# Wide-head attention of a four-layer decoder: four score banks, and the turning of a tile moved ahead of the product before it

## The chip, the cores and the metric

One core of a Trainium2 chip runs the whole program. The metric is the device time of one execution in microseconds. TensorE multiplies matrices, VectorE and ScalarE read its results out of PSUM (8 banks of 128 partitions x 512 float32), GpSimd does small side work, and SyncE starts the DMA transfers.

## The reference, cut to what matters

Twelve sublayers (attention, cross attention and feed-forward, four times) act on four sequences of 512 tokens of width 256. Four of them hold an attention whose head is "wide", that is a single head over 256 or 64 columns. All four have this core, in float32:

```python
scores = jnp.einsum('bqd,bkd->bqk', q, k) * scale      # 512 x 512 for each sequence
scores = jnp.where(mask, scores, -inf)                 # causal, by valid keys, or no mask
attn = jax.nn.softmax(scores, axis=-1)
y = jnp.einsum('bqt,btd->bqd', attn, v)
```

`L0_attn` is causal with width 256, `L0_ffn` is causal with width 64 (its attention sits between a mixture of projections and a mixture of outputs), `L1_xattn` has no mask and width 256, and `L3_xattn` masks keys and has width 256.

## The kernel before, in words

The program walks over the four sequences ("batches") one after another: nine early sublayers and the routing of the tenth for each batch, then a routed expert stage for all, then the last three sublayers for each batch. Every stage is a block in which each engine has its own instruction list and all engines meet at the end of the block; so a block lasts as long as its longest chain. `wide_attention` is one such block. It is called in `L0_attn`, `L0_ffn`, `L1_xattn` and `L3_xattn`, for 4 batches, so 16 times in all.

In a call, the 512 queries are four tiles t = 0 to 3 of 128 rows. `span[t]` is the number of keys that a tile looks at: 512, or 128, 256, 384 and 512 for the causal callers. For a tile there are six steps:

- the scores, on TensorE (line 354): one or two float32 products into PSUM bank t % 2. The trace shows a float32 product as two instructions, so a tile of width 256 has four, each with its load of the stationary side;
- the maximum of each row, on VectorE (line 384 without a mask, 395 with one; for `L3_xattn` line 389 multiplies by the key mask first). With a mask it also writes the masked scores into SBUF;
- the exponential with the row sum, on ScalarE (line 420), from the bank or from the masked scores, into `probs`;
- the turning (TensorE transposes of 128x128, line 366) of the tile's `span[t]`/128 chunks of `probs` into bank 2 + t % 2;
- the copy of that bank into `probs_t`, on VectorE (line 405);
- the product with the values, on TensorE (line 374), into bank 4 + t % 2, two instructions for each chunk, and then the finish on VectorE, which divides by the sum (line 408 has made its reciprocal) and adds or stores (lines 809, 977, 1034, 1957 in the callers).

Below, s0 to s3 are the scores, T0 to T3 the turnings and W0 to W3 the products with the values. `probs`, `scores`, `kept` and `probs_t` have two buffers each. The order is written out by hand. TensorE's list reads s0 s1 T0 W0 s2 T1 W1 s3 T2 W2 T3 W3. VectorE's reads maximum 0, maximum 1, copy 0, finish 0, maximum 2, copy 1, finish 1, maximum 3, copy 2, finish 2, copy 3, finish 3. Each W waits for its copy, and the copy of tile t stands on VectorE behind the maximum of tile t + 1:

```python
score(0)
for t in range(NT):
    if t + 1 < NT:
        score(t + 1)
    pe.wait_ge(probs_done, t + 1)      # then the turning of tile t
    ...
    pe.wait_ge(copied_done, t + 1)     # then its product with the values
```

After the block come a block of the caller or the next `layernorm`, which starts the load of the weights of the sublayer after it.

Of the kernel before, what the change touches and what calls it, by code (L numbers as in the profile page):

```python
# [21 lines left out]
ALU = mybir.AluOpType  # L22
ACT = mybir.ActivationFunctionType
AX = mybir.AxisListType

B, T, D, P = 4, 512, 256, 128
NT, NC = T // P, D // P
# [295 lines left out]

def wide_attention(net, q, k, values, width, causal, finish, keep=None, gone=None):

    masked = causal or keep is not None  # L330
    with ExitStack() as ctx:
        probs = net.sbuf("probs", [P, 2, T], ctx=ctx)
        scores = net.sbuf("scores", [P, 2, T], ctx=ctx) if masked else None
        kept = net.sbuf("kept", [P, 2, T], ctx=ctx) if keep is not None else None
        probs_t = net.sbuf("probs_t", [P, 2, T], ctx=ctx)
        nmax = net.sbuf("nmax", [P, NT], ctx=ctx)
        total = net.sbuf("total", [P, NT], ctx=ctx)
        inverse = net.sbuf("inverse", [P, NT], ctx=ctx)
        span = [(t + 1) * P if causal else T for t in range(NT)]
        with net.block() as (block, sem):  # L340
            scores_done, kept_done, max_done, probs_done = sem("scores"), sem("kept"), sem("maximum"), sem("exp")
            turned_done, copied_done, out_done = sem("transposed"), sem("transpose copied"), sem("p @ v")
            inverse_done, tile_done = sem("1/sum"), sem("tile written")

            @block.tensor
            def _(pe):
                def score(t):
                    if t >= 2:
                        if masked:
                            pe.wait_ge(max_done, t - 1)  # L350
                        else:
                            pe.wait_ge(probs_done, t - 1)
                    for i, (a, b) in enumerate(zip(q, k)):
                        mm = pe.matmul(net.psum[:, t % 2, 0:span[t]], a[:, t * P:(t + 1) * P], b[:, 0:span[t]],  # L354
                                       start=i == 0, stop=i == len(q) - 1)
                    mm.then_inc(scores_done, 1)

                score(0)
                for t in range(NT):
                    if t + 1 < NT:  # L360
                        score(t + 1)
                    pe.wait_ge(probs_done, t + 1)
                    if t >= 2:
                        pe.wait_ge(copied_done, t - 1)
                    for c in range(span[t] // P):
                        mm = pe.transpose(net.psum[:, 2 + t % 2, c * P:(c + 1) * P],
                                          probs[:, t % 2, c * P:(c + 1) * P], net.ident)
                    mm.then_inc(turned_done, 1)
                    pe.wait_ge(copied_done, t + 1)
                    if t >= 2:  # L370
                        pe.wait_ge(tile_done, t - 1)
                    n = span[t] // P
                    for c in range(n):
                        mm = pe.matmul(net.psum[:, 4 + t % 2, 0:width], probs_t[:, t % 2, c * P:(c + 1) * P],
                                       values(c), start=c == 0, stop=c == n - 1)
                    mm.then_inc(out_done, 1)

            @block.vector
            def _(dve):
                def maximum(t):  # L380
                    dve.wait_ge(scores_done, t + 1)
                    src = net.psum[:, t % 2, 0:span[t]]
                    if not masked:
                        dve.tensor_reduce(nmax[:, t:t + 1], src, AX.X, ALU.max, negate=True).then_inc(max_done, 1)
                        return
                    if t >= 2:
                        dve.wait_ge(probs_done, t - 1)
                    if keep is not None:
                        dve.tensor_tensor(kept[:, t % 2, :], src, keep, ALU.mult).then_inc(kept_done, 1)
                        dve.wait_ge(kept_done, t + 1)  # L390
                        src, mask = kept[:, t % 2, :], gone
                    else:
                        mask = net.causal[:, BANK - span[t]:BANK]

                    dve.tensor_tensor_reduce(scores[:, t % 2, 0:span[t]], src, mask, -1.0, 3e38, ALU.add, ALU.min,
                                             nmax[:, t:t + 1]).then_inc(max_done, 1)

                maximum(0)
                for t in range(NT):
                    if t + 1 < NT:  # L400
                        maximum(t + 1)
                    dve.wait_ge(turned_done, t + 1)
                    if t >= 2:
                        dve.wait_ge(out_done, t - 1)
                    dve.tensor_copy(probs_t[:, t % 2, 0:span[t]], net.psum[:, 2 + t % 2, 0:span[t]])\
                       .then_inc(copied_done, 1)
                    dve.wait_ge(probs_done, t + 1)
                    dve.reciprocal(inverse[:, t:t + 1], total[:, t:t + 1]).then_inc(inverse_done, 1)
                    dve.wait_ge(inverse_done, t + 1)
                    dve.wait_ge(out_done, t + 1)  # L410
                    finish(dve, t, net.psum[:, 4 + t % 2, 0:width], inverse[:, t:t + 1]).then_inc(tile_done, 1)

            @block.scalar
            def _(act):
                for t in range(NT):
                    act.wait_ge(max_done, t + 1)
                    if t >= 2:
                        act.wait_ge(turned_done, t - 1)
                    src = scores[:, t % 2, 0:span[t]] if masked else net.psum[:, t % 2, 0:span[t]]
                    act.activation(probs[:, t % 2, 0:span[t]], src, ACT.Exp, bias=nmax[:, t:t + 1],  # L420
                                   scale=-1.0 if masked else 1.0, accum_out=total[:, t:t + 1]).then_inc(probs_done, 1)

def stack_pairs(net, jobs, qs, ks, v, values, vbias, rope=None):
# [352 lines left out]
def L0_attn(net, W, x, xn, xc, **_):  # L779

    with ExitStack() as ctx:
# [26 lines left out]
        def finish(dve, t, ps, inverse):  # L808
            return dve.scalar_tensor_tensor(out=x[:, t, :], in0=ps, scalar=inverse, in1=x[:, t, :],
                                            op0=ALU.mult, op1=ALU.add)  # L810
        wide_attention(net, [q[:, c, :] for c in range(NC)], [k[:, c, :] for c in range(NC)],
                       lambda c: v[:, c, :], D, True, finish)

# [5 lines left out]
def L0_ffn(net, W, x, xn, xc, parts, **_):  # L819

    with ExitStack() as ctx:
# [154 lines left out]
        def finish(dve, t, ps, inverse):  # L976
            return dve.tensor_scalar(attn[:, t, :], ps, inverse, None, ALU.mult)
        wide_attention(net, [qk[:, 0, :]], [qk[:, 1, :]], lambda c: qkv[:, c, 2, :], MIXD, True, finish)

        mixed = lasting("mixed", [P, 2, MIX, MIXD])  # L980
# [38 lines left out]
def L1_xattn(net, W, x, xn, xc, cc, **_):  # L1019

    with ExitStack() as ctx:
        q = net.sbuf("q", [P, NC, T], ctx=ctx)
        k = net.sbuf("k", [P, NC, T], ctx=ctx)
        v = net.sbuf("v", [P, NT, D], ctx=ctx)
        o = net.sbuf("o", [P, NC, D, 2], ctx=ctx)
        table = []
        for c in range(NC):
            table.append(cols_out("dve", W["wq"], D, xc, c * P, q[:, c, :], ("scalar", W["bq"][:, c:c + 1], D ** -0.5, ALU.add, ALU.mult)))
            table.append(cols_out("act", W["wk"], D, cc, c * P, k[:, c, :], ("act", ACT.Identity, W["bk"][:, c:c + 1], 1.0)))
        table += [rows_out(alternate(t), cc, t, W["wv"], D, 0, D, v[:, t, :], copied(alternate(t)), W["bv"]) for t in range(NT)]  # L1030
        products(net, table)

        def finish(dve, t, ps, inverse):
            return dve.tensor_scalar(o[:, t % 2, :, t // 2], ps, inverse, None, ALU.mult)
        wide_attention(net, [q[:, c, :] for c in range(NC)], [k[:, c, :] for c in range(NC)],
                       lambda c: v[:, c, :], D, False, finish)
        add_output(net, x, o[:, :, :, :].rearrange("p c f r -> p c (f r)"), NC, P, W["wo"])
# [1407 lines left out]
```

## Time and profile before

| | |
|---|---|
| three runs | 4296.89, 4298.70 (median), 4308.47 us |
| the profiled execution | 4299.54 us, span of its instructions 4297.7 us |
| TensorE busy, loads busy | 79%, 50% of the span |
| VectorE, ScalarE, GpSimd busy | 48%, 27%, 9% |
| mean granted TensorE clock | 0.888 of full speed |

No engine is busy all the time; the program is a chain of blocks. The busy shares are means over blocks with different limits, so a block has to be read by itself: in the timeline of one call, and in the table of busy times by stretch, which also gives the granted TensorE clock (1.00 is 2.4 GHz, 0.50 is 1.2 GHz; a stretch with both lies between).

### The profile page before, as it was taken

Reading aid. Unit: us, or ns where it says so; the run is one execution under the profiler, and the core shown is the slowest. Engines: PE = TensorE matmul, PEld = TensorE weight load, DVE = VectorE, ACT = ScalarE, POOL = GpSimd, SP = SyncE. Lnnn points to the kernel's source line nnn. Section 1 sums busy time; section 2 is a strip of 40 time slices with the busy share of each in tenths; the row PEclk is TensorE's granted clock in tenths of the full one; section 3 lists DMA queues with packets and bytes.
Section 4 is the critical chain, followed back from the end, with each engine's and each line's share of the span. In section 5 each row is a group of like instructions: output and inputs, shape, how many; then the busy total and the mean of one; then the engine's idle time right before and its main releaser. Section 6 shows DMA issues by size and latency. Waiting matters only on the chain. (4 is left out here: it accounts for less than half of the span.)

```text
span 4297.7 us, 49457 instructions
## 1 busy us (share of the span) xinstructions
PE 3401.4 (79%) x18289; PEld 2170.2 (50%) x18289; DVE 2078.9 (48%) x4553; ACT 1146.9 (27%) x2199; POOL 401.3 (9%) x381
## 2 busy tenths in 40 slices
PE   4778689678869967887986778798595888877888
PEld 3364555436455544645454455544593454454545
DVE  3655445465545546555555654554113435344353
ACT  1413125141223414122341312243131213112121
POOL 0010101010010101001010100101102000010100
PEclk9888899888889978898997979899797998989989
DMA  4000100200010010001001000100682110102011
GB/s 163 13 13 21 63 11 1 86 13 13 21 63 11 17 70 13 13 20 63 11 28 59 13 13 23 61 10 33 246 306 97 51 41 7 78 8 84 8 51 38
DMA packets 53212, 209.27 MB, mean 49 GB/s; under 512 B 4977, under 2 KB 37617, under 8 KB 41329
## 3 DMA queue, kind: packets, MB, share of 16 engines
q1 hardware_dynamic: 48128, 198.85, 12.5%
q0 software_dynamic: 1536, 4.20, 0.3%
q8 instruction: 157, 2.57, 0.2%
q10 hardware_dynamic: 3312, 3.02, 0.2%
q14 instruction: 79, 0.64, 0.0%
HBM read 186.89 MB, written 19.16 MB: 48 GB/s over the span
## 5 line engine op out<-in xcount | busy, mean ns | idle before, releaser
L643 DVE TENSOR_REDUCE nmax<-psum 128x1 f32<-128x512 f32 (+3 forms) x768 | 392.2, 553 | 135.6 <-PE psum L579 91.5
L685 ACT ACTIVATE probs<-psum 128x1024 f32<-128x1024 f32 (+3 forms) x384 | 304.4, 814 | 431.0 <-PE psum L607 290.0
L108 PE MATMUL psum<-select 128*128 128x512 f32 x1016 | 280.2, 431 | 82.9 <-PEq L120 82.9
L574 PE MATMUL psum<-ks,qs 64*128 64x512 f32 (+3 forms) x768 | 211.1, 546 | 139.5 <-DVE nmax L643 123.5
L108 PEld LDWEIGHTS psum<-select 128*128 128x128 f32 x1016 | 205.3, 208 | 156.9 <-issue 113.3
L316 ACT ACTIVATE xc<-psum 128x256 f32<-128x256 f32 x152 | 54.5, 389 | 790.1 <-PE psum L309 790.1
L265 POOL TENSOR_SCALAR rstd<-mean_var 128x4 f32<-128x4 f32 x48 | 10.9, 228 | 2491.5 <-DVE mean_var L290 2491.5
L574 PEld LDWEIGHTS psum<-ks,qs 64*128 64x128 f32 x768 | 89.0, 227 | 290.2 <-DVE nmax L643 269.5
L1490 ACT ACTIVATE exps<-exps,nmax 128x512 f32<-128x512 f32 x256 | 183.4, 717 | 71.4 <-DVE nmax L1436 71.0
L1436 DVE CUSTOM_DVE_ANT_0 exps<-psum,mrows 128x512 f32<-128x512 f32 x256 | 166.1, 689 | 67.9 <-PE psum L1383 64.6
L602 PE MATMUL psum<-qs,ks 64*128 64x512 f32 (+3 forms) x768 | 165.0, 435 | 7.8 <-ACT probs L685 7.8
L618 PE MATMUL psum<-probs,v 128*32 128x512 f32 (+3 forms) x1536 | 166.4, 506 | 3.3 <-ACT probs L685 2.5
L1394 PE MATMUL psum<-consts,exps 128*128 128x128 f32 x1024 | 138.9, 279 | 3.8 <-DVE arena L1444 1.5
L1394 PEld LDWEIGHTS psum<-consts,exps 128*128 128x128 f32 x1024 | 109.5, 141 | 55.9 <-ACT exps L1490 39.8
L1405 PE MATMUL psum<-arena,v 128*64 128x512 f32 x512 | 134.8, 608 | 3.6 <-ACT arena L1503 3.2
L746 DVE RECIPROCAL inv<-psum 128x512 f32<-128x512 f32 x16 | 53.7, 3358 | 166.8 <-PE psum L721 166.8
L2045 PE MATMUL psum<-xc,arena 128*128 128x512 f32 x256 | 123.6, 606 | 4.1 <-PEq L120 4.1
L354 PE MATMUL psum<-k,q 128*128 128x512 f32 (+3 forms) x192 | 92.9, 625 | 37.8 <-PEq L120 37.8
L738 PE MATMUL psum<-arena,scaled 128*128 128x256 f32 x512 | 120.0, 382 | 0.0
L293 DVE TENSOR_SCALAR xn<-x,mean_var,rstd 128x256 f32<-128x256 f32 x192 | 85.3, 508 | 70.7 <-POOL rstd L267 70.7
L199 PE MATMUL psum<-arena,proj 128*128 128x256 f32 x512 | 111.5, 380 | 5.8 <-PEq L120 5.8
L738 PEld LDWEIGHTS psum<-arena,scaled 128*128 128x128 f32 x512 | 96.0, 190 | 38.0 <-issue 15.3
(371 smaller groups left out, 6700.9 us busy)
## 6 DMA issues: line engine op xcount, KB each, us to landing
arena<-in_w SPq DMA_DIRECT2D x23, 1028.0 KB, 5.0
arena<-in_w SPq DMA_DIRECT2D x23, 1024.0 KB, 5.2
arena<-in_pack_L_ffn SPq DMA_DIRECT2D x4, 5184.5 KB, 15.5
arena<-in_pack_L_xattn SPq DMA_DIRECT2D x4, 4744.0 KB, 13.9
arena<-in_pack_L_ffn SPq DMA_DIRECT2D x4, 4120.0 KB, 13.1
arena<-in_pack_L_attn SPq DMA_DIRECT2D x5, 2432.0 KB, 9.2
arena<-in_pack_L_attn SPq DMA_DIRECT2D x9, 1280.0 KB, 5.5
arena<-ternary SPq DMA_DIRECT2D x4, 2056.0 KB, 7.8
```

What stands on the lines that cost most here:

```text
L108: pe.matmul(self.psum[:, bank, :], self.select[:, 0, :], self.select[:, 0:BANK // P, :], start=True, stop=True)
L574: mm = pe.matmul(net.psum[:, bank_of(s + j), 0:w], qs[half, p, qt * P:(qt + 1) * P], ks[half, p, 0:w], start=True, stop=not causal)
L602: mm = pe.matmul(net.psum[:, 2 + 2 * (n % 2) + j, lo:T], ks[half, p, kt * P:(kt + 1) * P], qs[half, p, lo:T], start=True, stop=not causal)
L618: mm = pe.matmul(net.psum[u * PITCH:(u + 1) * PITCH, 6, lo:T], v[:, kt, 4 * g + u, :], probs[:, (2 * m + u // 2) % buffers, u % 2, lo:T], ...
L643: dve.tensor_reduce(nmax[:, p, qt, n % 2:n % 2 + 1], net.psum[:, bank_of(s), 0:w], AX.X, ALU.max, negate=True).then_inc(row_read, 1)
L685: act.activation(probs[:, n % buffers, :, lo:T], net.psum[:, first:first + 2, lo:T], ACT.Exp, scale=scale)\
L738: mm = pe.matmul(net.psum[:, 4 + t, 0:D], scaled[:, c, t * P:(t + 1) * P], w[:, c * D:(c + 1) * D], start=c == 0, stop=c == GROUPS - 1)
L1394: mm = pe.transpose(net.psum[:, 4 + j, kt * P:(kt + 1) * P], e[:, m % ring, kt * P:(kt + 1) * P], net.ident)
L1405: mm = pe.matmul(net.psum[half, 6, :], v[:, kt, 2 * p + j, :], turned[p % 2][:, kt, j, :], start=kt == 0, stop=kt == NT - 1, tile_position ...
L1436: dve.tensor_tensor_reduce(e[:, m % ring, :], net.psum[:, 2 * (u % 2) + j, :], mrows[:, u % NT, :], -DK ** -0.5, 1e20, ALU.add, ALU.min, n ...
L1490: act.activation(e[:, m % ring, :], e[:, m % ring, :], ACT.Exp, bias=nmax[:, m % ring:m % ring + 1], scale=-1.0, accum_out=total[:, p % 2, ...
L2045: mm = pe.matmul(net.psum[:, n % 2, :], W["down"][:, at:at + P], xc[:, c, :], start=c == 0, stop=c == 1)
```

## The change

- The scores of the four tiles have a bank each (0, 1, 6 and 7), so the waits of the scores for a free bank are gone. `probs` and `scores` have four buffers in place of two, so the waits of the exponential and of the maximum for a free buffer are gone (of the latter the masked product, `kept`, keeps one, on VectorE itself).
- TensorE's list becomes s0 s1 s2 s3 T0 T1 W0 T2 W1 T3 W2 W3.
- VectorE's list becomes maximum 0 to 3, copy 0, copy 1, finish 0, copy 2, finish 1, copy 3, finish 2, finish 3.
- The number and shapes of the instructions that compute stay as they are. `probs_t` and the banks 2 to 5 stay doubled, with their waits.

```diff
-                def score(t):
-                    if t >= 2:
-                        if masked:
-                            pe.wait_ge(max_done, t - 1)
-                        else:
-                            pe.wait_ge(probs_done, t - 1)
...
+                    for i, (a, b) in enumerate(zip(q, k)):
+                        mm = pe.matmul(net.psum[:, score_banks[t], 0:span[t]], a[:, t * P:(t + 1) * P], b[:, 0:span[t]],
...
-                score(0)
-                for t in range(NT):
-                    if t + 1 < NT:
-                        score(t + 1)
+                def turn(t):
                     pe.wait_ge(probs_done, t + 1)
                     if t >= 2:
                         pe.wait_ge(copied_done, t - 1)
...
+                def weigh(t):
                     pe.wait_ge(copied_done, t + 1)
                     if t >= 2:
                         pe.wait_ge(tile_done, t - 1)
...
+                for t in range(NT):
+                    score(t)
+                turn(0)
+                for t in range(NT):
+                    if t + 1 < NT:
+                        turn(t + 1)
+                    weigh(t)
...
-                maximum(0)
-                for t in range(NT):
-                    if t + 1 < NT:
-                        maximum(t + 1)
+                def copy(t):
                     dve.wait_ge(turned_done, t + 1)
                     if t >= 2:
                         dve.wait_ge(out_done, t - 1)
...
+                for t in range(NT):
+                    maximum(t)
+                copy(0)
+                for t in range(NT):
+                    if t + 1 < NT:
+                        copy(t + 1)
                     dve.wait_ge(probs_done, t + 1)
...
-                    if t >= 2:
-                        act.wait_ge(turned_done, t - 1)
```

## Rows read from the trace of the kernel before

**Rows 1.** Calls by stretch: us, busy PE, PEld, DVE, ACT, POOL (instructions), PEclk, DMA, GB/s.

```profile
71.12:85.95 14.83, 11.25 (x46) 7.42 (x46) 5.86 (x20) 2.62 (x8) 0.00 (x0) 1.00 0.01 2
809.60:827.20 17.60, 14.06 (x46) 9.13 (x46) 5.70 (x20) 2.62 (x8) 0.00 (x0) 0.81 0.00 0
...
274.50:290.60 16.10, 13.29 (x38) 8.10 (x38) 5.36 (x20) 2.62 (x8) 0.00 (x0) 0.50 0.00 0
...
436.44:457.55 21.11, 16.93 (x64) 10.62 (x64) 7.37 (x16) 3.12 (x8) 0.00 (x0) 1.00 0.00 0
...
3413.24:3438.75 25.51, 19.23 (x64) 11.42 (x64) 10.19 (x24) 3.26 (x8) 0.00 (x0) 0.91 0.00 1
```

**Rows 2.** Waits by who waited for whom: total us, times, longest us.

```profile
PEld psum L374 <- DVE probs_t L405: 75.3, 64, 1.9
```

**Rows 3.** Timeline, a call of L1_xattn: start, us, engine, line, op [idle before <-releaser].

```profile
438.47 0.69 DVE L384 TENSOR_REDUCE nmax<-psum 128x1 f32<-128x512 f32 x1 [2.31 <-PE psum L354]
...
440.18 0.69 DVE L384 TENSOR_REDUCE nmax<-psum 128x1 f32<-128x512 f32 x1 [1.02 <-PE psum L354]
440.79 0.68 DVE L405 COPY probs_t<-psum 128x512 f32<-128x512 f32 x1
...
441.52 1.59 PEld L374 LDWEIGHTS psum<-v,probs_t 128*128 128x128 f32 x8 [1.08 <-DVE probs_t L405]
...
443.14 0.41 PEld L354 LDWEIGHTS psum<-k,q 128*128 128x128 f32 x2
...
443.64 0.48 DVE L1034 TENSOR_SCALAR o<-psum,inverse 128x256 f32<-128x256 f32 x1 [2.10 <-PE psum L374]
...
451.71 1.59 PEld L374 LDWEIGHTS psum<-v,probs_t 128*128 128x128 f32 x8 [1.18 <-DVE probs_t L405]
...
453.33 0.57 PEld L366 LDWEIGHTS psum<-consts,probs 128*128 128x128 f32 x4
...
454.95 1.59 PEld L374 LDWEIGHTS psum<-v,probs_t 128*128 128x128 f32 x8 [1.05 <-DVE probs_t L405]
```

**Rows 4.** Timeline, a call of L3_xattn.

```profile
3419.16 0.69 DVE L389 TENSOR_TENSOR kept<-psum,keep 128x512 f32<-128x512 f32 x1 [0.68 <-PE psum L354]
...
3420.51 0.69 DVE L405 COPY probs_t<-psum 128x512 f32<-128x512 f32 x1
...
3421.24 1.59 PEld L374 LDWEIGHTS psum<-ct,probs_t 128*128 128x128 f32 x8 [1.45 <-DVE probs_t L405]
...
3436.15 1.59 PEld L374 LDWEIGHTS psum<-ct,probs_t 128*128 128x128 f32 x8 [1.04 <-DVE probs_t L405]
```

**Rows 5.** Timeline, the first call of L0_attn.

```profile
72.74 0.43 DVE L395 CUSTOM_DVE_ANT_0 scores<-psum,consts 128x256 f32<-128x256 f32 x1 [0.57 <-PE psum L354]
...
73.12 0.29 DVE L405 COPY probs_t<-psum 128x128 f32<-128x128 f32 x1
...
73.47 0.30 PEld L374 LDWEIGHTS psum<-v,probs_t 128*128 128x128 f32 x2 [0.57 <-DVE probs_t L405]
...
83.36 1.59 PEld L374 LDWEIGHTS psum<-v,probs_t 128*128 128x128 f32 x8 [1.04 <-DVE probs_t L405]
```

**Rows 6.** The start of its second call by stretch, columns as in Rows 1.

```profile
809.90:816.70 6.80, 6.29 (x16) 3.90 (x16) 1.49 (x7) 1.09 (x4) 0.00 (x0) 0.50 0.00 1
```

**Rows 7.** Timeline, the first call of L0_ffn.

```profile
276.18 0.42 DVE L395 CUSTOM_DVE_ANT_0 scores<-psum,consts 128x256 f32<-128x256 f32 x1 [0.55 <-PE psum L354]
...
286.20 0.87 PEld L366 LDWEIGHTS psum<-consts,probs 128*128 128x128 f32 x4
...
288.25 1.78 PEld L374 LDWEIGHTS psum<-qkv,probs_t 128*128 128x128 f32 x8 [1.18 <-DVE probs_t L405]
```

**Rows 8.** The block after that call: its transposes in the timeline.

```profile
292.22 6.46 PE L1000 MATMUL psum<-consts,mixed 128*128 128x128 f32 x32 [2.00 <-DVE mixed L990]
```

**Rows 9.** Stretches of that block and behind it, columns as in Rows 1.

```profile
292.20:297.90 5.70, 5.68 (x27) 5.66 (x28) 3.55 (x3) 3.26 (x6) 0.00 (x0) 0.50 0.00 0
297.90:301.00 3.10, 2.11 (x13) 1.77 (x12) 0.00 (x0) 1.42 (x3) 0.00 (x0) 1.00 0.02 5
```

More of the change, by code:

```diff
@@ L330, in wide_attention @@
     masked = causal or keep is not None
+    score_banks = (0, 1, 6, 7)
     with ExitStack() as ctx:
-        probs = net.sbuf("probs", [P, 2, T], ctx=ctx)
-        scores = net.sbuf("scores", [P, 2, T], ctx=ctx) if masked else None
+        probs = net.sbuf("probs", [P, NT, T], ctx=ctx)
+        scores = net.sbuf("scores", [P, NT, T], ctx=ctx) if masked else None
         kept = net.sbuf("kept", [P, 2, T], ctx=ctx) if keep is not None else None
@@ L347, in score @@
                 def score(t):
-                    if t >= 2:
-                        if masked:
-                            pe.wait_ge(max_done, t - 1)
-                        else:
-                            pe.wait_ge(probs_done, t - 1)
                     for i, (a, b) in enumerate(zip(q, k)):
-                        mm = pe.matmul(net.psum[:, t % 2, 0:span[t]], a[:, t * P:(t + 1) * P], b[:, 0:span[t]],
+                        mm = pe.matmul(net.psum[:, score_banks[t], 0:span[t]], a[:, t * P:(t + 1) * P], b[:, 0:span[t]],
                                        start=i == 0, stop=i == len(q) - 1)
                     mm.then_inc(scores_done, 1)
-                score(0)
-                for t in range(NT):
-                    if t + 1 < NT:
-                        score(t + 1)
+                def turn(t):
                     pe.wait_ge(probs_done, t + 1)
@@ L365, in _ @@
                     for c in range(span[t] // P):
-                        mm = pe.transpose(net.psum[:, 2 + t % 2, c * P:(c + 1) * P],
-                                          probs[:, t % 2, c * P:(c + 1) * P], net.ident)
+                        mm = pe.transpose(net.psum[:, 2 + t % 2, c * P:(c + 1) * P], probs[:, t, c * P:(c + 1) * P], net.ident)
                     mm.then_inc(turned_done, 1)
+                def weigh(t):
                     pe.wait_ge(copied_done, t + 1)
@@ L381, in maximum @@
                     dve.wait_ge(scores_done, t + 1)
-                    src = net.psum[:, t % 2, 0:span[t]]
+                    src = net.psum[:, score_banks[t], 0:span[t]]
                     if not masked:
@@ L385, in maximum @@
                         return
-                    if t >= 2:
-                        dve.wait_ge(probs_done, t - 1)
                     if keep is not None:
+                        if t >= 2:
+                            dve.wait_ge(max_done, t - 1)
                         dve.tensor_tensor(kept[:, t % 2, :], src, keep, ALU.mult).then_inc(kept_done, 1)
@@ L393, in maximum @@
                         mask = net.causal[:, BANK - span[t]:BANK]
-                    dve.tensor_tensor_reduce(scores[:, t % 2, 0:span[t]], src, mask, -1.0, 3e38, ALU.add, ALU.min,
+                    dve.tensor_tensor_reduce(scores[:, t, 0:span[t]], src, mask, -1.0, 3e38, ALU.add, ALU.min,
                                              nmax[:, t:t + 1]).then_inc(max_done, 1)
-                maximum(0)
-                for t in range(NT):
-                    if t + 1 < NT:
-                        maximum(t + 1)
+                def copy(t):
                     dve.wait_ge(turned_done, t + 1)
@@ L416, in _ @@
                     act.wait_ge(max_done, t + 1)
-                    if t >= 2:
-                        act.wait_ge(turned_done, t - 1)
-                    src = scores[:, t % 2, 0:span[t]] if masked else net.psum[:, t % 2, 0:span[t]]
-                    act.activation(probs[:, t % 2, 0:span[t]], src, ACT.Exp, bias=nmax[:, t:t + 1],
+                    src = scores[:, t, 0:span[t]] if masked else net.psum[:, score_banks[t], 0:span[t]]
+                    act.activation(probs[:, t, 0:span[t]], src, ACT.Exp, bias=nmax[:, t:t + 1],
                                    scale=-1.0 if masked else 1.0, accum_out=total[:, t:t + 1]).then_inc(probs_done, 1)
```

## The prediction

> **What bounds the kernel now.** I read the table by stretch first, cut at the 16 calls of the changed block, to see how long the calls are, at which clock they run and whether one engine fills them. Four rows stand for the four callers, and one more for the case in which the clock differs [rows 1]: about 14.8 us for `L0_attn` (two of its four calls; the other two last 17.6), 16.1 for `L0_ffn`, 21.1 for `L1_xattn`, 25.5 for `L3_xattn`. Weighted by four calls each that is about 316 us, 7% of the program; the change can touch only these. Within a call no engine is full. In the `L1_xattn` call TensorE is busy 16.93 of 21.11 us, VectorE 7.37, ScalarE 3.12.
>
> The waits by who waited for whom then name the idle stretches: all 64 products with the values wait for the copy of their turned tile, 75.3 us in total [rows 2]. The timeline of one call shows why [rows 3]. Copy 0 starts at 440.79, right behind maximum 1 (440.18), although the turned tile had been ready; W0 follows 0.73 us after the copy's start. Only after W0 do the scores of tile 2 go out (443.14), since they stand behind it in TensorE's list. So in each round TensorE runs scores and turning, stops for maximum and copy, and runs the product. The chain that ends the block is s0, s1, maximum 1, copy 0, W0, s2, T1, maximum 2, copy 1, W1 and so on: TensorE work and VectorE work in a row, not side by side.
>
> **The change part by part.** Everything after the load of W3 (its product, the last finish, the end of the block) is as before. So I work out, for one call of each caller, when W3 starts to load, and compare it with the old start.
>
> *The scores moved ahead.* Four scores without a break: a tile of 512 keys and width 256 takes 1.71 us, the distance of maximum 1 from maximum 0 (440.18 - 438.47) [rows 3]. All four maxima now stand ahead of copy 0 on VectorE, and this is the wait that the change adds: behind copy 0 in the queue stands everything else of VectorE, and W0 waits for it. Its cost is in the walk below, as W0 starts later than before. The exponentials run on ScalarE, which is busy 3.12 us of the call, beside this.
>
> *The turning moved ahead of the product.* Each turning of four chunks loads in 0.57 us, eight loads of a product take 1.62 us to the next instruction (451.71 to 453.33) [rows 3]. Once W0 has started, the list T2 W1 T3 W2 W3 runs on if every copy is in time. Copy 2 stands behind finish 0, and finish t starts 2.12 us after its product began to load (441.52 to 443.64) and takes 0.48; then 0.73 from copy to load: 3.33 us after W0, whereas W2 comes 1.62 + 0.57 + 1.62 + 0.57 = 4.38 after W0. Copy 3 in the same way: 3.33 after W1, whereas W3 comes 1.62 + 0.57 + 1.62 = 3.81 after it. So TensorE has no wait, with 0.5 us to spare at the tightest place for 512 keys. In the causal callers, whose early tiles are short, the room is about 0.1 us.
>
> *`L1_xattn`* [rows 3]: maximum 3 starts at 438.47 + 3 x 1.71 = 443.60. Copy 0 follows 0.61 later (as 440.79 follows 440.18), at 444.21, and W0 0.73 later, at 444.94. T0 and T1, 1.14 us together, lie beside that. From W0 to W3: three products and two turnings, 3 x 1.62 + 2 x 0.57 = 6.00, so W3 at 450.94 in place of 454.95. Gain 4.0 us.
>
> *`L3_xattn`* [rows 4]: VectorE needs 1.35 us for a tile's mask product and maximum (3419.16 to 3420.51), less than the 1.71 of a score, so scores set the pace. The mask product of tile 3 starts at 3419.16 + 2 x 1.71 = 3422.58, copy 0 at 3423.93, W0 0.73 later at 3424.66, W3 at 3430.66 in place of 3436.15. Gain 5.5 us.
>
> *`L0_attn`* [rows 5]: maximum 1 at 72.74. Tile 2 has three quarters of the columns (1.28, an estimate from the 1.71), tile 3 all: maximum 3 at 75.73. Copy 0 at + 0.61 = 76.34, W0 at + 0.35 (73.12 to 73.47) = 76.69. Up to W3 there are 2 + 4 + 6 = 12 loads of products at 1.62 / 8 and 3 + 4 = 7 of turnings at 0.57 / 4: 3.43. W3 at 80.12 in place of 83.36. Gain 3.2 us. Two of the four calls have half the clock over 6.8 us from their start [rows 6], which makes them 17.60 - 14.83 = 2.8 longer [rows 1]; I let the loss stand and give them the same gain.
>
> *`L0_ffn`* runs at half the clock all through [rows 1]. A single product for a tile's scores (width 64) at half the clock costs as two at full, so again 1.28 and 1.71 for tiles 2 and 3: maximum 3 at 276.18 + 2.99 = 279.17 [rows 7], W0 0.61 + 0.35 later at 280.13. The loads take 0.22 here (1.78 / 8 and 0.87 / 4 [rows 7]): 19 x 0.22 = 4.18. W3 at 284.31 in place of 288.25. Gain 3.9 us.
>
> *Costed at nothing*: the waits dropped (TensorE's for a score bank, ScalarE's for a buffer) take no engine time; their stalls are in the walk. The wider buffers add no instruction. No DMA is moved in the list; the next weights are asked for one sublayer ahead, by the `layernorm` that now starts 3 to 6 us sooner. If a load were late by that, the gain of the call would be lost, but no more.
>
> Sum: 4 x (4.0 + 5.5 + 3.2 + 3.9) = 66.4 us. From the profiled 4299.5 that leaves 4233; the median of the three runs is 0.8 us lower, so **4232 us**. What is late next in the call: W0, which waits for maximum 3 and copy 0 (TensorE idle some 0.3 us in `L1_xattn`, 1.3 in `L3_xattn`), and behind it TensorE itself.
>
> *The clock, bounded from both sides.* No row shows a call in the new order. Upwards: `L0_ffn` could come to full clock since TensorE no longer pauses. 27 loads from W0 on and 32 transposes of the next block, which take 6.46 us [rows 8], would go from 0.22 and 0.20 to about 0.14 (0.57 / 4): 2.2 + 1.9 us a call, 16 in all. Downwards: the shift of all later work can put a half-clock stretch where there was none; it costs 2.8 us each [rows 1], and eight more of them 22 us. I take nothing, as three of the four callers are at 0.91 to 1.00 in most rows [rows 1]. These bounds give 4216 and 4254.
>
> A rule against the change: 5.70 us in which TensorE ran nothing but transposes began at clock 0.50 and were followed by 1.00 [rows 8, 9], so transposes count as work for the clock here. The Trainium skill, "TensorE: Matmul & The Clock Gate", section "Part 4: PE-mode transpose", says otherwise: full rate does not engage for transposes, since they don't count as busy in the same way. By the row the sum stays; by the page it would be the rival "clock lost" below. The trace disagrees with the page.
>
> **The rivals.**
> - *Clock gain*, 4216: the upper bound above. For it: TensorE's list in `L0_ffn` runs without a pause from W0 to W3. Against: after the call there is a pause of 2.0 us [rows 8] that stays.
> - *The VectorE chain*, 4268: if W2 and W3 came only after finish, copy and load of the tiles before (2.12 + 0.48 + 0.73 = 3.33 a step in place of 2.19), two steps lose 2.3 a call, 36 in 16 calls. For it: finish 0 stands ahead of copy 2. Against: W1 lies between, with the room worked out above.
> - *Clock lost between s3 and W0*, 4266: only T0, T1 and the idle time lie there; if they dropped the clock, each of the 12 calls at full clock would lose 2.8 us, 34 in all. Against: in the old order TensorE pauses over a microsecond before each W [rows 3] at clock 1.00.
> - *Slower*, 4313: the clock falls at the same place and stays at half up to the end of the call. W0 to W3 would double: 7.62 in eight calls and 5.05 in four, together 81 us, 14 more than the gain. It decides from the point where over 66 / 81 = 82% of these stretches are at half. Against: the known half stretch ends after 6.8 us although TensorE pauses within it [rows 6].
> - *Nothing*, 4299: a wait that isn't in the trace keeps the old rounds. Nothing in the diff would do so.
>
> **How the numbers follow.** Forecast 0.72, clock gain 0.12, VectorE chain 0.07, clock lost 0.03, slower 0.03, nothing 0.03. The forecast's own range is 4218 to 4248 (the walk within 10%, and some half-clock stretches more or fewer); with the bounds of the clock the range is 4210 to 4254, which leaves out the last four cases, 0.16. About 0.3%, 13 us, is what a measurement of this kernel can tell from no change: faster 0.94 (the first four), same 0.03, slower 0.03.
>
> **What would show it.** In the profile after, a call of `L1_xattn` should last about 17.1 us, of `L3_xattn` 20.0, of the shorter `L0_attn` 11.6 and of `L0_ffn` 12.2. Copy 0 should stand right behind maximum 3, W0 should be the only product that waits for its copy, so the total of that wait should fall from 75 us to some 20, and four scores should go out at 1.71 a tile. It would be wrong if W2 or W3 wait for their copies, if the clock row of the calls falls below that of before, or if the time goes back in the blocks behind the calls.

## The result, and the profile after

The changed kernel takes 4219.39 us (median; 4217.98 to 4224.96), the kernel before took 4296.89 beside it; the ratio is 0.9818, with a 95% interval of 0.9803 to 0.9833. That is 77.5 us less, where 66.4 were forecast: 4219.4 in place of 4232, inside the range of 4210 to 4254. The profiled execution took 4219.39 us, its span is 4217.6 and its mean granted clock 0.892.

The same view by stretch as in [rows 1], of the kernel after (stretch, its length, busy time of PE, PEld, DVE, ACT, POOL with instructions, clock, DMA): two calls of `L0_attn`, then one each of `L0_ffn`, `L1_xattn` and `L3_xattn`, each cut after its last finish.

```profile
70.64:83.85 13.21, 11.92 (x46) 8.51 (x46) 5.81 (x20) 2.62 (x8) 0.00 (x0) 0.87 0.00 1
797.89:811.10 13.21, 11.92 (x46) 8.63 (x46) 5.81 (x20) 2.62 (x8) 0.00 (x0) 0.87 0.00 1
272.62:284.44 11.82, 11.25 (x38) 8.38 (x38) 5.21 (x20) 2.62 (x8) 0.00 (x0) 0.50 0.00 0
429.18:446.35 17.17, 16.03 (x64) 10.67 (x64) 7.38 (x16) 3.11 (x8) 0.00 (x0) 1.00 0.00 0
3360.26:3380.45 20.19, 18.32 (x64) 11.58 (x64) 10.18 (x24) 3.26 (x8) 0.00 (x0) 0.88 0.01 1
```

TensorE now fills the calls: in `L1_xattn` it is busy 16.03 of 17.17 us, where it was 16.93 of 21.11 [rows 1]. VectorE and ScalarE do the same work as before. The wait of [rows 2], 75.3 us in 64 pieces, has become this row of the waits view (total, times, longest):

```profile
PEld psum L364 <- DVE probs_t L400: 14.8, 16, 1.5
```

One wait is left in each call, that of W0. The timeline of a call of `L1_xattn`, to be held against [rows 3] (start, length, engine, line, operation; in brackets the idle time before it and what ended it):

```profile
431.20 0.69 DVE L382 TENSOR_REDUCE nmax<-psum 128x1 f32<-128x512 f32 x1 [2.31 <-PE psum L346]
...
436.35 0.69 DVE L382 TENSOR_REDUCE nmax<-psum 128x1 f32<-128x512 f32 x1 [1.02 <-PE psum L346]
436.96 1.28 DVE L400 COPY probs_t<-psum 128x512 f32<-128x512 f32 x2
...
437.69 1.59 PEld L364 LDWEIGHTS psum<-v,probs_t 128*128 128x128 f32 x8 [0.74 <-DVE probs_t L400]
...
439.31 0.57 PEld L355 LDWEIGHTS psum<-consts,probs 128*128 128x128 f32 x4
...
439.86 1.60 PEld L364 LDWEIGHTS psum<-v,probs_t 128*128 128x128 f32 x8
...
441.48 0.58 PEld L355 LDWEIGHTS psum<-consts,probs 128*128 128x128 f32 x4
441.97 0.48 DVE L1032 TENSOR_SCALAR o<-psum,inverse 128x256 f32<-128x256 f32 x1 [1.01 <-PE psum L364]
442.02 3.32 PEld L364 LDWEIGHTS psum<-v,probs_t 128*128 128x128 f32 x16
...
442.37 0.68 DVE L400 COPY probs_t<-psum 128x512 f32<-128x512 f32 x1
```

Maximum 3 starts 5.15 us after maximum 0 (three tiles at 1.72), copy 0 stands right behind it, W0 follows 0.73 later, and from there T2, W1, T3, W2 and W3 load without a break. The copies come in time: copy 3 starts at 442.37 and would let W3 load at 443.10, and TensorE comes to W3 at 442.02 + 1.62 = 443.64.

For what follows, a call is counted from the load of its first score to the end of its last product, in the timeline. The 16 calls sum to 307.6 us before and 240.9 after, 66.7 less. The rest of the span goes from 3990.1 to 3976.7, 13.4 less, although its instructions are the same. So two things are to be explained: which part of the change gives the 66.7, and where the 13.4 come from.

### The profile page after: what moved, and what is told of

The parts are those of the page before. It is cut to its first block and busy times, and to the rows that moved or that the text cites. A ratio compares the mean times of both kernels' runs of the same rounds, so it can differ in the third digit from the quotient of the medians.

```text
span 4217.6 us, 49409 instructions
## 1 busy us (share of the span) xinstructions
PE 3372.7 (80%) x18289; PEld 2170.9 (51%) x18289; DVE 2078.1 (49%) x4553; ACT 1146.6 (27%) x2199; POOL 401.5 (10%) x381
## 3 DMA queue, kind: packets, MB, share of 16 engines
q1 hardware_dynamic: 48128, 198.85, 12.6%
```

## The experiments

A series is a set of runs taken together; the kernel before ran in each, with medians of 4296.9 to 4305.6 us, and the ratios are to it. This table has the medians (single times for three), the sum of the calls and the rest of the span in the profile:

| kernel | time, us | 16 calls | rest |
|---|---|---|---|
| before (two profiles) | 4296.9, 4294.5 | 307.6, 307.4 | 3990.1, 3988.7 |
| after (two profiles) | 4219.4, 4223.1 | 240.9, 240.9 | 3976.7, 3979.8 |
| scores first, turning not ahead | 4274.8 | 295.6 | 3980.8 |
| turning ahead, two score banks | 4222.2 | 236.6 | 3985.0 |
| after, end of `L3_xattn` 1.2 us later | 4231.3 (single) | 238.8 | 3990.5, of which 4.9 added |
| after, end of `L3_xattn` 2.4 us later | 4237.8 (single) | 240.2 | 3995.8, of which 9.8 added |
| after, more VectorE work ahead of the copies | 4231.1 (single), 4232.4 | 244.3, 244.3 | 3984.8, 3988.7 |
| after, with dummy products ahead | 4202.7 | 211.2 | 3986.0 |
| turning ahead, two banks, dummy products | 4206.2 | 223.9 | 3978.3 |
| after, more dummy products | 4190.8 | 207.0 | 3981.7 |
| turning ahead, two banks, more dummy products | 4202.3 | 211.7 | 3986.9 |

### Scores first, without the turning ahead

```diff
-                turn(0)
                 for t in range(NT):
-                    if t + 1 < NT:
-                        turn(t + 1)
+                    turn(t)
                     weigh(t)
...
-                copy(0)
                 for t in range(NT):
-                    if t + 1 < NT:
-                        copy(t + 1)
+                    copy(t)
```

> Four score banks as in the change, but each tile is turned, copied and weighed in turn: T0 W0 T1 W1 T2 W2 T3 W3, and VectorE has copy t, finish t. Theory (the turning moved ahead carries the gain): copy t+1 now stands behind finish t, so a round is 2.12 + 0.48 + 0.73 = 3.33 us at 512 keys, and W3 starts 9.99 us after W0 in place of 6.00. L1_xattn then ends where it did before, L3_xattn 1.5 us sooner, L0_ffn 0.7, L0_attn about even: some 8 us less than before in all, about 4289, within 10 us for the clock. Rival (the scores in four banks carry it): at least half of the 77 us stay, 4258 or less.

Measured: 4274.77 us, ratio 0.9939 (0.9918 to 0.996), 26 us less than before. The calls give 12.0 of it, against some 8 expected: `L3_xattn` 1.7 a call, `L0_ffn` 0.9, `L1_xattn` 0.3, `L0_attn` 0.1 in the mean. The total was missed, because the rest of the span was 9 us shorter too; the rival, at least half of the gain, was missed as well. The timeline of its `L1_xattn` call shows the round that was worked out:

```profile
445.10 1.59 PEld L364 LDWEIGHTS psum<-v,probs_t 128*128 128x128 f32 x8 [1.18 <-DVE probs_t L398]
...
447.21 0.48 DVE L1028 TENSOR_SCALAR o<-psum,inverse 128x256 f32<-128x256 f32 x1 [2.10 <-PE psum L364]
447.61 0.68 DVE L398 COPY probs_t<-psum 128x512 f32<-128x512 f32 x1
...
448.34 1.59 PEld L364 LDWEIGHTS psum<-v,probs_t 128*128 128x128 f32 x8 [1.05 <-DVE probs_t L398]
```

Product, finish, copy, product: 3.24 us a round, with TensorE's loads idle over a microsecond before each W. Four banks alone leave this chain as it is.

### The turning ahead, with two score banks

On the kernel before, with its buffers and waits; VectorE's list in the same order (maximum 0, 1, copy 0, then maximum t + 2, copy t + 1, finish t).

```diff
-                score(0)
-                for t in range(NT):
-                    if t + 1 < NT:
-                        score(t + 1)
+                score(0)
+                score(1)
+                turn(0)
+                for t in range(NT):
+                    if t + 2 < NT:
+                        score(t + 2)
+                    if t + 1 < NT:
+                        turn(t + 1)
+                    weigh(t)
```

> Two score banks and two buffers with all waits of the kernel before, but the turning moved ahead of the product: s0 s1 T0 s2 T1 W0 s3 T2 W1 T3 W2 W3, VectorE maximum 0, 1, copy 0, maximum 2, copy 1, finish 0, maximum 3, copy 2, finish 1, copy 3, finish 2, 3. Theory (the order matters, not the banks): the scores of tile 2 fill TensorE while copy 0 runs, W3 of L1_xattn starts 14.2 us after the first score in place of 14.5 after the change, L3_xattn is the same, L0_attn and L0_ffn gain 0.3 to 0.5 a call: 4215, within 6. Rival (two banks hold the order up): a wait for a bank or buffer comes back, at least 2 us a call, 4250 or more.

Measured: 4222.17 us, ratio 0.9817 (0.9797 to 0.9838); the changed kernel in the same series 0.9824 (0.9803 to 0.9845). So the order gives the whole gain, and the four banks are not needed for it. The orders of TensorE and VectorE were changed together; no run has one without the other. The calls are 4.3 us shorter than after the change, as expected in sum (the time missed the range of 4209 to 4221 by 1 us), though not caller by caller: `L1_xattn` 15.9 in place of 16.6, `L3_xattn` 18.9 in place of 19.6 and `L0_attn` 12.0 in place of 12.6 in the mean, but `L0_ffn` 12.3 in place of 11.4. The rest of the span took the gain back. In `L3_xattn` turnings wait for their exponential here, as in this row of T3:

```profile
3376.77 0.42 PEld L363 LDWEIGHTS psum<-consts,probs 128*128 128x128 f32 x4 [0.60 <-ACT probs L435]
```

### Both kernels once more

> The changed kernel once more. In the first profiles the 16 calls (first score load to the end of the last product) sum to 307.6 us before and 240.9 after, a gain of 66.7; the rest of the span is 3990.1 and 3976.7, a gain of 13.4 that lies outside the calls. Theory (where the half-clock stretches fall outside the calls differs from one execution to the next): the calls repeat within 3 us, the rest moves by 5 us or more. Rival (the shorter calls make the blocks behind them faster each time): the rest comes out at 3976.7 within 2 us.

> The kernel before once more. Theory (half-clock stretches outside the calls differ from one execution to the next): the calls sum to 307.6 within 4 us, the rest moves by 5 us or more from 3990.1. Rival (a steady difference): the rest is 3990.1 within 2 us.

Measured: 4223.09 and 4294.53 us. The sums of the calls agree within 0.2 us. The rest is 3979.8 in place of 3976.7, and 3988.7 in place of 3990.1. It moves by 3.1 after the change and by 1.4 before it, less than the 5 us that luck was to bring; the 3.1 are more than the rival's 2 us.

Two profiles of a kernel that come out alike don't show that nothing is drawn. In the series of these runs the executions of the kernel before take 4289 to 4309 us. Its four `L0_attn` calls last 14.24, 17.12, 17.12 and 14.24 us in one profile and 18.25, 14.24, 15.43 and 15.51 in the other, so that the sums agree is chance. And the two kernels of the next section differ from the changed kernel only from the first `L3_xattn` call on. Up to it, the changed kernel (twice) and these two run the same instructions, but the views by stretch are 7.7 us apart:

```profile
0.00:3360.26 3360.26, 2656.67 (x14673) 1721.48 (x14673) 1711.38 (x3740) 965.66 (x1878) 340.40 (x320) 0.89 0.14 52
0.00:3363.49 3363.49, 2658.87 (x14673) 1720.76 (x14674) 1711.29 (x3740) 965.29 (x1878) 340.08 (x320) 0.89 0.14 52
0.00:3365.61 3365.61, 2662.14 (x14673) 1723.85 (x14673) 1711.25 (x3740) 965.39 (x1878) 340.03 (x320) 0.89 0.14 52
0.00:3367.94 3367.94, 2668.15 (x14673) 1729.05 (x14674) 1711.17 (x3740) 965.71 (x1878) 340.11 (x320) 0.88 0.14 52
```

Outside the calls TensorE is at half the clock there for 697, 711, 718 and 728 us by the clock record, in the order of the lengths. So over this part of the program the theory is borne out: the same instructions got more or less half clock from one execution to another. (The four come from three series, which may add to it.)

The part from the first `L3_xattn` call on does repeat. Outside its calls it takes 784.5 and 784.1 us before and 778.9 and 778.8 after, and the timeline shows where the 5.5 us lie. In a block behind each `L3_xattn` call a chain on VectorE takes 11.4 us while TensorE runs 36 products beside it; then TensorE turns VectorE's result and runs five more products, for which the rest of the block waits. Before the change a half-clock stretch falls on these products in some calls and ahead of the chain in the others, and either costs about 1.4 us; one of them is so in each of the eight calls of both profiles. After the change it falls, in all eight, on the products beside VectorE, where it costs nothing. (With the turning ahead and two score banks it falls on the five products in all four calls, and this part takes 784.1 us again.) The five products behind the first of these calls, before and after:

```profile
3462.38:3465.90 3.52, 3.52 (x5) 1.67 (x6) 0.00 (x0) 1.25 (x2) 0.00 (x0) 0.56 0.00 0
3404.07:3406.06 1.99, 1.99 (x5) 1.02 (x6) 0.00 (x0) 1.24 (x2) 0.00 (x0) 1.00 0.00 0
```

So of the 13.4 us outside the calls some 5.5 are steady. The other 8 lie ahead of the first `L3_xattn` call, where the changed kernel's own instructions spread as widely.

### The end of a call later

Behind the last finish of the `L3_xattn` calls, with n = 2 and n = 4:

```diff
+                for i in range(late):
+                    dve.tensor_copy(probs[:, i, :], net.psum[:, 2, :])
```

> The changed kernel, with two more VectorE copies of a bank behind the last finish of the L3_xattn calls (4 of the 16), 1.2 us in all, that nobody reads. From the first score of one such call to that of the next it took 255.8 to 256.0 us before, 252.6 with the scores first alone and 249.2 after, so the steps are 3.4 us although the calls themselves became 1.7 and 5.4 shorter. Theory (the half-clock stretches in the blocks behind the call take up the difference, since where they fall depends on when the call ends): the time from call to call stays at 249.2 or goes to 252.6, and isn't 250.4. Rival (the rest is the same from call to call, whatever the call does): 249.2 + 1.2 = 250.4.

> The same with four more copies, 2.4 us. Theory: the time from call to call is 252.6 (or still 249.2). Rival: 251.6.

Measured, from call to call: 249.28, 249.18 and 252.02 us with 1.2 us added; 252.38, 250.95 and 251.02 with 2.4 added. Adding 1.2 us costs nothing twice and 2.8 us once; adding 2.4 costs 3.2 once and 1.8 twice. The changed kernel has 248.97 to 249.24 in six such ways, so the rest isn't the same whatever the call does. Of the values that I expected, 249.2 and 252.6, four of the six are near; the two at 251.0 are neither these nor the rival's 251.6, so the rule of fixed steps fell. The total times, 4231.27 and 4237.77, are no price of the later end: each is of a single run, and 5.4 and 7.7 us of its distance to the first profile of the changed kernel lie ahead of the first edited instruction.

### More VectorE work in the chain of the copies

```diff
                 def copy(t):
+                    if t >= 2:
+                        dve.tensor_tensor(extra[:, :], net.causal, net.causal, ALU.add)
                     dve.wait_ge(turned_done, t + 1)
```

> The changed kernel with one more VectorE operation of 512 columns (0.61 us to the next) ahead of copy 2 and of copy 3 in every call, in the chain from a finish through the copy to the next product; its output is read by nobody. Theory (TensorE sets the end of the call, VectorE has room: after the change copy 2 of L1_xattn is through 1.1 us before TensorE comes to W2, copy 3 0.5 before W3): L1_xattn and L3_xattn become 0.1 us longer a call, L0_ffn 0.1, L0_attn 0.5. Rival (the VectorE chain sets the end): both copies come 0.61 later and each call is 1.2 us longer.

> The changed kernel with one more VectorE operation ahead of copy 2 and copy 3, once more, with rounds. In its profile the calls were 3.4 us longer than after the change (all of it in L0_attn), the rest of the span 5.0 to 8.1 us longer although the instructions there are the same. Theory (the end of a call decides where half-clock stretches fall behind it, in the same way in every execution): the median is again some 10 us above that of the changed kernel, 4229 to 4233, and the rest 3984 within 2. Rival (the rest is luck of one execution): the median is 3.4 us above, 4223 to 4226, and the rest 3978.

Measured: `L1_xattn` 16.57 and `L0_ffn` 11.44 us a call as without it, `L3_xattn` between 19.50 and 19.64, and `L0_attn` 0.86 longer (13.47). The room in the chain is there as worked out, and used up only in `L0_attn`: W2 of it now waits for its copy (it doesn't in the changed kernel):

```profile
808.12 0.55 DVE L403 COPY probs_t<-psum 128x384 f32<-128x384 f32 x1
808.72 1.16 PEld L365 LDWEIGHTS psum<-v,probs_t 128*128 128x128 f32 x6 [0.33 <-DVE probs_t L403]
```

The time, however, is 4231.11 us, and 4232.38 (4231.14 to 4234.87) in the second series: some 10 us above the changed kernel in other series, and not 3.4. These 10 us aren't clear of noise. The ratio to the kernel before is 0.984 (0.9824 to 0.9857), and the changed kernel's own 0.9818 and 0.9824 have intervals that overlap it; and in the first of these two series the kernels of the section above need as long as this one outside the calls, 3204.8 and 3205.4 us against 3205.9 up to the first `L3_xattn` call. In the second series the rest was to be 3984 within 2 and is 3988.7, a miss.

What does show clearly is one part of it, the way from an `L0_attn` call to the next `L0_ffn` call. Behind the second to fourth calls it lasts 190.4 to 190.7 us here, in six of six, and 188.3 to 189.2 in the four profiles of the kernels whose call ends as after the change, in twelve of twelve. Before the change it is 190.1 to 190.4 in three of eight and 188.6 to 189.1 in the others. Three kernels, the same instructions behind the second call, in three stretches by the same offsets (before, after, this one):

```profile
826.73:834.00 7.27, 4.60 (x20) 2.98 (x20) 4.84 (x14) 1.09 (x3) 3.48 (x5) 0.99 0.78 290
834.00:841.00 7.00, 5.93 (x15) 4.83 (x16) 0.52 (x2) 0.77 (x2) 1.83 (x3) 0.53 0.71 304
841.00:1017.00 176.00, 133.54 (x611) 79.16 (x609) 121.10 (x205) 53.20 (x65) 19.71 (x8) 0.86 0.02 8
```

```profile
810.51:817.80 7.29, 4.62 (x20) 2.98 (x20) 4.85 (x14) 1.09 (x3) 3.49 (x6) 1.00 0.78 296
817.80:824.10 6.30, 5.24 (x17) 4.41 (x18) 0.51 (x2) 0.77 (x2) 1.82 (x3) 0.73 0.76 330
824.10:998.80 174.70, 132.20 (x608) 78.44 (x608) 121.08 (x205) 53.20 (x65) 19.73 (x8) 0.86 0.02 8
```

```profile
813.13:820.42 7.29, 4.64 (x21) 2.98 (x20) 4.85 (x14) 1.09 (x3) 3.49 (x6) 0.99 0.77 287
820.42:828.00 7.58, 6.51 (x17) 5.24 (x18) 0.51 (x2) 0.77 (x2) 1.82 (x3) 0.56 0.66 283
828.00:1003.50 175.50, 133.10 (x608) 78.67 (x607) 121.03 (x205) 53.19 (x65) 19.72 (x8) 0.86 0.02 8
```

In the second stretch TensorE has 15 to 17 products. It runs them at a mean clock of 0.73 in the changed kernel, and at 0.53 and 0.56 in the other two, and the stretch takes 6.30 us against 7.00 and 7.58. (The stretch of the kernel before is cut two instructions shorter.) That is 1.3 of the 2.1 us between the changed kernel and this one; the other 0.8 lie in the third stretch. The stretch at half the clock itself, in the changed kernel and in this one:

```profile
818.55:821.96 3.41, 3.10 (x7) 2.53 (x8) 0.00 (x0) 0.38 (x1) 1.11 (x2) 0.50 1.05 454
820.33:827.16 6.83, 5.67 (x13) 4.49 (x14) 0.60 (x2) 0.56 (x2) 1.83 (x3) 0.50 0.73 314
```

The call ended 0.86 us later, and the half clock behind it lasts twice as long. This holds throughout: of the 40 such ways in the ten profiles without added dummy products, the 29 with 3.4 us at half the clock behind the call last 188.3 to 189.5 us, and the 11 with 6.8 us last 190.1 to 191.1.

### Dummy products ahead of the calls

TensorE idles in the blocks ahead of `L0_attn`, `L0_ffn` and `L3_xattn`; here it multiplies there, into a bank that nobody reads: 10 products in the rotation of `L0_attn`, 30 behind the projections of `L0_ffn`, 14 while `L3_xattn` makes its masks.

```diff
+            @block.tensor
+            def _(pe):
+                net.keep_warm(pe, 10)
...
+                net.keep_warm(pe, 30, bank=0, after=(weighed_done, 20))
...
+                net.keep_warm(pe, 14)
```

> The changed kernel with dummy products on TensorE in the three blocks ahead of calls where TensorE has nothing to do: 10 in the rotation of L0_attn, 30 at the end of the projections of L0_ffn, 14 while L3_xattn makes its masks. Their results are read by nobody. Theory (the calls of these three lose time to the half clock with which they begin): L0_attn 11.0 us from the first score to the end of the last product in place of 12.6, L0_ffn about 8.7 in place of 11.4, L3_xattn 17.4 in place of 19.6, together 26 us less in 12 calls, and with the turning ahead of and behind L0_ffn some 33: about 4188. Rival (the clock at the start of a call is of no account, since VectorE and ScalarE set the pace there): the calls as they are, 4220.

Measured: 4202.70 us, ratio 0.978 (0.9757 to 0.9804). `L0_attn` takes 10.93 us in all four calls and `L3_xattn` 17.31, as expected (11.0 and 17.4); `L0_ffn` 6.93 in three calls, less than the 8.7 expected, and 11.11 in one. The calls lose 29.7 us against the changed kernel. The rest is 9 us longer than in its first profile, and the total was missed by 15; part of the 9 may be the series, in which the same instructions up to the first `L3_xattn` call took 5 to 8 us longer than in that profile. The odd call and its neighbour in the view by stretch show what is different, the clock:

```profile
992.60:1004.11 11.51, 10.92 (x38) 8.06 (x38) 5.22 (x20) 2.62 (x8) 0.00 (x0) 0.52 0.00 0
271.31:278.64 7.33, 6.28 (x38) 4.66 (x38) 5.07 (x20) 2.62 (x8) 0.00 (x0) 1.00 0.00 0
```

> Both findings together: two score banks with the order s0 s1 T0 s2 T1 W0 s3 T2 W1 T3 W2 W3, and dummy products ahead of the calls of L0_attn, L0_ffn (33 in place of 30, since one of the four calls there had still begun at half the clock) and L3_xattn. Theory (the gains of the calls add up): from the first score to the end of the last product L1_xattn 15.9 us, L0_attn 10.9, L0_ffn 7, L3_xattn 16.9, together 203 in place of the 211.2 of the dummy products alone; the rest of the span at 3986 as there gives 4190, within 8 for the half-clock stretches elsewhere. Rival (the order of the two lists doesn't matter once the clock is full, since VectorE then sets the pace): 211 in the calls, 4199.

Measured: 4206.22 us (ratio 0.9781, 0.9765 to 0.9798), a miss. Three callers came out as expected (15.90, 10.94 and 17.09 us), but `L0_ffn` began at the full clock and fell back to half in all four calls, 11.9 to 12.2 us each, for 224 in the calls in place of 203. The two last kernels try the pause that was left, with five more products in the block that turns the queries and keys of `L0_ffn` (`warm=5` there):

```diff
-def products(net, table, name="products"):
+def products(net, table, name="products", warm=0):
...
+            net.keep_warm(pe, warm)
```

> The changed kernel with the dummy products of e5_warm (10, 30, 14), and 5 more in the block that turns the queries and keys of L0_ffn, where TensorE waits some 2 us for ScalarE between its transposes and the first scores. Theory (that pause let the clock fall in one call of four): all four calls of L0_ffn last 6.9 us, the calls sum to 207, and the time is some 5 us below that of e5_warm, 4198, within 6. Rival (the clock falls for another reason): again one or more calls of L0_ffn at 11 us, 4203.

> The order with two score banks (s0 s1 T0 s2 T1 W0 s3 T2 W1 T3 W2 W3) and the same dummy products (10, 30, 5, 14). Theory: L0_ffn at full clock, about 7 us a call in place of 12, the calls sum to 203, some 20 us less than in e6_turn_ahead_warm, 4186, within 8. Rival (in this order TensorE pauses at the head of the L0_ffn call, which lets the clock fall whatever stands ahead): L0_ffn again near 12 us, 4206.

Measured: on the changed kernel 4190.81 us, ratio 0.9745 (0.9715 to 0.9774), with all four `L0_ffn` calls at 6.93 us and the calls at 207.0, as expected; the time is 1 us below the range of 4192 to 4204. It is the fastest of all. One odd call in four against none is thin evidence for the pause as the cause; the other order shows more, where the calls lasted 11.9 to 12.2 us without the five products. On the other order 4202.29 us (0.9767, 0.9745 to 0.979) in place of 4186: `L0_ffn` 8.35, 10.75, 8.35 and 8.50 us. Two of them by stretch:

```profile
273.31:282.05 8.74, 6.90 (x38) 4.62 (x38) 5.20 (x20) 2.62 (x8) 0.00 (x0) 1.00 0.01 2
994.84:1005.98 11.14, 10.17 (x38) 7.19 (x38) 5.29 (x20) 2.62 (x8) 0.00 (x0) 0.64 0.00 0
```

The rival has a part in the second, where the clock fell to half within the call (0.64 over it). But the first is at 1.00 and still takes 8.74 us, 1.4 more than with four scores in a row (7.32 below): with scores between the turnings the short tiles of `L0_ffn` leave pauses. The four callers in the fastest kernel, by stretch:

```profile
71.94:83.47 11.53, 10.23 (x46) 7.42 (x46) 5.81 (x20) 2.62 (x8) 0.00 (x0) 1.00 0.00 1
273.51:280.83 7.32, 6.28 (x38) 4.65 (x38) 5.07 (x20) 2.62 (x8) 0.00 (x0) 1.00 0.00 0
426.75:443.92 17.17, 16.03 (x64) 10.67 (x64) 7.38 (x16) 3.12 (x8) 0.00 (x0) 1.00 0.00 1
3338.36:3356.25 17.89, 16.03 (x64) 10.67 (x64) 10.17 (x24) 3.26 (x8) 0.00 (x0) 1.00 0.00 1
```

All are at 1.00, and the call of `L0_ffn`, 11.82 us at 0.50 after the change, takes 7.32. The Trainium skill ("TensorE: Matmul & The Clock Gate", "Part 1: The HAM clock gate") says that the throttled state is the default and that activity releases it. These rows agree with the release: with products in the idle stretch ahead of it, the call begins and stays at 1.00.

## Why the prediction was right, point by point

- *The chain of the old order* was read rightly. Scores first alone left rounds of 3.24 us at each product and gave 12.0 us in the calls; the turning ahead alone, with two banks, gave 71.0, more than both together (66.7). The prediction priced the two edits together and didn't say which carries it; the runs say that the second does.
- *The walk, caller by caller.* `L1_xattn` 17.17 us by stretch (17.1 forecast), `L3_xattn` 20.19 (20.0). `L0_ffn` 11.82 (12.2), as the 0.22 us a load at half the clock was a little too high (W3 3.79 us behind W0, 4.18 forecast). W0 waits longer than the 0.3 us in `L1_xattn` and 1.3 in `L3_xattn` that the prediction named: 0.74 and 1.49. `L0_attn` 13.21 in all four calls, where 11.6 in two and 14.4 in the others were forecast. In sum the calls gained 66.7 us against 66.4.
- *The clock of `L0_attn`* is a term that was mis-sized, twice and in opposite directions. "I let the loss stand and give them the same gain" is wrong for all four calls of the first two profiles: the two at full clock before now start at half (0.87 over the call), gaining 1.6 and not 3.2, and the two that lost 2.8 now lose less, gaining 4.4. That they balance is chance. Which calls start at half is not a property of the call either: the second profile of the kernel before has other ones, and in the kernel with 1.2 us added at the end of `L3_xattn`, which is the changed kernel up to there, the first call runs at 1.00 and takes 10.93 us in place of 12.62. One of the prediction's own signs of being wrong came, as the clock row of a call fell below that of before (1.00 to 0.87). With dummy products ahead, the call takes 11.53 us by stretch at clock 1.00: the 11.6 of the walk was the time at full clock.
- *The VectorE chain* has the room that was worked out: an operation of 0.61 us more ahead of two copies cost nothing in `L1_xattn` and `L0_ffn`, and 0.86 us in `L0_attn`, where the prediction saw 0.1 us of room. That rival, and "nothing", are ruled out.
- *Clock lost between s3 and W0* and *slower* are ruled out: all four `L1_xattn` calls stay at 1.00 with only turnings and an idle 0.74 us between their scores and W0, and in `L0_attn` and `L3_xattn` of the first profile the half clock of the start ends 3.6 to 4.7 us after the first score and doesn't come back in the call.
- *Clock gain* by the new order alone did not come: all four `L0_ffn` calls stayed at 0.50. The size given to it, 2.2 us in a call, was too small: at the full clock the call is 4.5 us shorter.
- *Blocks behind the calls.* "I take nothing" for the shift of half-clock stretches was the step of the sum that failed: of the 77.5 us the calls give 66.7, and about 11 come from outside them, where the prediction had 0 (4219 in place of 4232; 1.8 us of that distance is the kernel before, 4296.9 here and 4298.7 on record). The range had room for it, but as a spread and not as a gain. The runs show two parts in its place. Some 5.5 us are steady: behind the `L3_xattn` calls the half clock fell, before the change, where the block's chain ran through it, and falls beside VectorE's work after it. The rest, 5 to 8 us, lies ahead of them and is not told apart from luck: the changed kernel's own instructions took 3360.3 to 3367.9 us there, and the kernel before has 3205.6 and 3204.6 outside the calls, the changed one 3197.8 to 3205.4. Time at half the clock outside the calls went the same way but doesn't give the amount: 864 us in both profiles before, 830 and 844 after, and 857 with scores first, whose rest of 3980.8 is nearly as short as after the change. Which end of a call is lucky could not be told ahead, and this stays open.

## What to carry to other kernels

In a chain of matmul, vector step, transpose, copy and matmul on engines that work in order, put the next tile's transpose ahead of this tile's product, and its copy ahead of this tile's finish; four score banks without that gave 12.0 us in the calls, and that without them 71.0. Price a move in such a kernel by walking one instance of the block to the start of its last product, and then check the room in the other engine's queue (here 0.1 to 1.1 us). Where a block begins after an idle stretch, look at its granted clock first: filling that stretch took another 33.9 us off the calls here (240.9 to 207.0) and some 29 off the time (4219.4 to 4190.8, in different series), over a third of what the change did. Before a difference of some 10 us between two such kernels is given a cause, look at how far executions of one of them are apart over the same instructions.

## What the runs showed of the hardware that was not expected

- The same instructions from the start to the first `L3_xattn` call took 3360.3, 3363.5, 3365.6 and 3367.9 us in four executions, with 697 to 728 us at half the clock outside the calls.
- With `L0_attn` calls that ended 0.86 us later, the stretch at half the clock behind the second to fourth of them lasted 6.8 us in place of 3.4, in six of six, and the way to the next `L0_ffn` call was 1.2 to 2.4 us longer.
- A stretch of 3.4 us at half the clock cost about 1.4 us behind an `L3_xattn` call where the block waited for TensorE's products, and nothing where it waited for VectorE.
- The same 38 TensorE instructions of an `L0_ffn` call took 11.82 us at clock 0.50 and 7.32 at 1.00, with the order of the lists unchanged.
